# Edge filters of every second four steps computed inside the one-head attention instead of in the filter stage

## The reference

```python
out_i = xw[etype, dst]
out_j = xw[etype, src]
alpha = leaky_relu(out_i @ Q + out_j @ K, 0.2)
alpha = _segment_softmax(alpha, dst, n)
msg = (out_j.reshape(-1, heads, out_ch) * alpha[..., None]).reshape(-1, heads * out_ch)
return segment_sum(msg, dst, num_segments=n) + b
```

```python
h1 = h @ aw_W + aw_b
C = 0.5 * (cos(edge_weight * (PI / CUTOFF)) + 1.0)
Wf = ssp(ssp(edge_attr @ m1_W + m1_b) @ m2_W + m2_b)      # ssp(x) = softplus(x) - log 2
Wf = Wf * C[:, None]
msg = h1[src] * Wf
agg = segment_sum(msg, dst, num_segments=n_nodes)
```

## Time and profile before

| | |
|---|---|
| median of three runs | 6127.67 us (6123.48 to 6130.93) |
| profiled execution, span from first to last instruction | 6128.0 us |
| busy: PE / DVE / ACT / POOL | 4062 / 3143 / 1987 / 3556 us |
| narrow attention, from its first `cuts` to its last add | 3485 to 4151 us |
| filter stage, from its first gather to its last add | 4338 to 5265 us |

### The profile page before, as it was taken

One profiled execution on the slowest core, in us unless ns is written; L12 is line 12 of the kernel. 1 busy time (PEld: TensorE's weight loads), 2 busy tenths in 40 slices (PEclk: granted clock), 3 DMA queues, 4 the chain that ended last, 5 costly groups with the idle time before them and its releaser, 6 DMA issues. The chain is left out here.

```text
span 6128.0 us, 77751 instructions
## 1 busy us (share of the span) xinstructions
PE 4062.0 (66%) x17164; PEld 2958.9 (48%) x17165; DVE 3143.4 (51%) x7175; ACT 1987.0 (32%) x4687; POOL 3556.1 (58%) x2851
## 2 busy tenths in 40 slices
PE   5599922596777769677677444445688888745553
PEld 5488811353555555355556333333455555533332
DVE  5577636522555542355554344445477777533334
ACT  0122200000665541266563122220477777400000
POOL 0244411277777725677773788865555555478884
PEclk9999966798887879788787655557799999866555
DMA  0000002234665534566552233333234343243332
GB/s 7 24 10 10 10 27 61 77 77 94 172 168 154 158 89 92 135 171 166 153 156 61 62 84 83 84 79 89 71 102 103 103 104 103 79 101 84 84 84 73
DMA packets 511546, 558.56 MB, mean 91 GB/s; under 512 B 302820, under 2 KB 394959, under 8 KB 511005
## 3 DMA queue, kind: packets, MB, share of 16 engines
q0 software_dynamic: 349600, 362.07, 24.5%
q1 hardware_dynamic: 158408, 187.29, 10.7%
q10 hardware_dynamic: 3250, 6.40, 0.4%
HBM read 460.45 MB, written 92.22 MB: 90 GB/s over the span
## 5 line engine op out<-in xcount | busy, mean ns | idle before, releaser
L1259 POOL DMA_INDIRECT sum_gx_sb<-scratch_xw,keep_k_row_step_sb x1272 | 1602.7, 1260 | 469.9 <-issue 351.3
L1372 PE MATMUL sum_a_ps<-sum_gx_sb,sum_sel_sb 125*125 125x258 f32 (+1 forms) x4320 | 1214.4, 445 | 539.5 <-ACT sum_gx_sb L1308 218.9
L1372 PEld LDWEIGHTS sum_a_ps<-sum_gx_sb,sum_sel_sb 125*125 125x125 f32 x4320 | 936.1, 242 | 732.2 <-issue 514.1
L1308 ACT ACTIVATE sum_gx_sb<-sum_gx_sb,sum_wt_sb 125x129 f32<-125x129 f32 x3312 | 981.8, 388 | 561.5 <-DVE sum_wt_sb L1501 527.2
L2473 POOL DMA_INDIRECT filter_gx_sb<-scratch_h,keep_k_src_step_sb x424 | 513.5, 1211 | 410.6 <-DVEq L2620 299.0
L1168 POOL DMA_INDIRECT scratch_grouped<-keep_k_value_sb,keep_k_place_sb x400 | 481.7, 1204 | 272.6 <-issue 137.1
L2917 POOL DMA_INDIRECT source_gx_sb<-scratch_h,source_grouped_sb x424 | 527.5, 1244 | 140.4 <-issue 117.5
L2929 PE MATMUL source_s_ps<-source_gx_sb,source_sel_sb 125*125 125x257 f32 x848 | 370.0, 612 | 310.8 <-DMA source_gx_sb<-scratch_h,source_grouped_sb 310.8
L2929 PEld LDWEIGHTS source_s_ps<-source_gx_sb,source_sel_sb 125*125 125x125 f32 x848 | 246.3, 304 | 434.5 <-issue 172.1
L2527 PE MATMUL filter_ps<-filter_m_sb,filter_h_sb 128*125 128x256 f32 x1728 | 403.9, 387 | 15.6 <-DVE filter_f_sb L2592 15.3
L2527 PEld LDWEIGHTS filter_ps<-filter_m_sb,filter_h_sb 128*125 128x125 f32 x1728 | 318.2, 189 | 141.9 <-issue 98.2
(11 more groups left out here) (513 smaller groups left out, 6861.5 us busy)
## 6 DMA issues: line engine op xcount, KB each, us to landing
scratch_hots<-sum_cuts_sb SPq DMA_DIRECT2D x108, 244.1 KB
filter_sel_sb<-scratch_hots SPq DMA_DIRECT2D x106, 244.1 KB
sum_gx_sb<-scratch_xw,keep_k_row_step_sb POOLq DMA_INDIRECT x1272
scratch_xw<-gate_xsb_sb SPq DMA_DIRECT2D x50, 253.9 KB
scratch_xw<-attend_xsb_sb SPq DMA_DIRECT2D x25, 507.8 KB
filter_ea_sb<-in_ea_t SPq DMA_DIRECT2D x436, 24.4 KB
filter_gx_sb<-scratch_h,keep_k_src_step_sb POOLq DMA_INDIRECT x424
source_gx_sb<-scratch_h,source_grouped_sb POOLq DMA_INDIRECT x424
```

The costliest lines, as they stand in the source:

```text
L1259: nc.gpsimd.indirect_dma_start(out=gx[:, q, j, :], out_offset=None, in_=table, in_offset=bass.IndirectOffsetOnAxis(ap=keep["row_step"][:, ...
L1308: last = nc.scalar.activation(here, here, ACT.Copy, scale=wt[q][:, h, j:j + 1])
L1372: last = mm(psa[b][0:P, half, 0:BF], sel[:, 0, p, j, :], gx[:, q, at, half * BF:(half + 1) * BF], **flags)
```

## The change

Half of the edge filters move. `PAIRS` = 106 pairs of steps (steps 4 to 7 of each eight, as two pairs) get their filters in the narrow attention, a pair in each of its 108 parts; SP stores them to a new buffer in HBM, `scratch_wf`. The filter stage then works in 53 turns of eight steps: the first four get their filters as before, the second four load theirs (`wf`).

In the narrow attention the pipeline for pair c is: SP loads its attributes two parts ahead (`filter_load`), PE makes the hidden layer of pair c and the filters of pair c - 2 after the sums of a part and before the link of the score chain (`filter_products`), ACT makes the logarithms of the hidden layer of c and the filters of c - 3 (`filter_logs`), two of a block's three sets before the exponential `weights(s + 1)` and one behind it, DVE makes the softplus sides of c - 1 and c - 4 and the bias of c - 2 after the part's add (`filter_sides`), and SP stores pair c - 5 (`filter_store`). The weights are loaded at the stage's start, and again in the filter stage as before. The loops of all engines in this stage now go over PEEL = 6 blocks, with six blocks ahead of the loop and six behind it. ACT loads one function table, with Exp and Ln, at the stage's start.

```diff
+def filter_products(nc, pe, fl, i, c):
+    mm, P2 = nc.tensor.matmul, 2 * P
+    if pair_runs(i, c):
+        pe.wait_ge(fl["e_in"][c % 3], i * (32 * ROUND_PAIRS // 3) + 32 * (c // 3 + 1))
+        if c >= 2:
+            pe.wait_ge(fl["h1_made"], i * ROUND_PAIRS + c - 1)
+        for o in range(2):
+            last = mm(fl["psh"][c % 2][:, o * P2:(o + 1) * P2], fl["m1"][0:51, 128 * o:128 * o + 128], fl["ea"][0:51, c % 3, :],
+                      start=True, stop=True)
+        last.then_inc(fl["hid"], 1)
+    u = c - 2
+    if pair_runs(i, u):
+        pe.wait_ge(fl["h1_made"], i * ROUND_PAIRS + u + 1)
+        if u >= 1:
+            pe.wait_ge(fl["f2_made"], i * ROUND_PAIRS + u)
+        for j in range(2):
+            for b in range(2):
+                last = mm(fl["psf"][0:P, j * D:(j + 1) * D], fl["h1"][u % 2][:, b * P2 + j * P:b * P2 + j * P + P], fl["m2"][:, b, :],
+                          start=(b == 0), stop=(b == 1))
+        last.then_inc(fl["filt"], 1)
+def filter_sides(nc, dve, fl, i, c):
...
+        vec.scalar_tensor_tensor(fl["h1"][u % 2][:], fl["psh"][u % 2][:, 0:4 * P], 0.0, fl["lgh"][u % 2][:], ALU.max,
+                                 ALU.add).then_inc(fl["h1_made"], 1)
...
+        vec.scalar_tensor_tensor(here, here, 0.0, fl["lgf"][u % 2][:], ALU.max, ALU.add).then_inc(fl["f_made"], 1)
...
+        dve.wait_ge(fl["filt"], i * ROUND_PAIRS + u + 1)
...
+            def block_with_filters(s, q, i, c, last=False):
+                scale(s, q)
+                filter_logs(nc, act, fl, i, c)
+                filter_logs(nc, act, fl, i, c + 1)
+                if not last:
+                    weights(s + 1)
+                filter_logs(nc, act, fl, i, c + 2)
...
                     with pe.If(tiles[p] > NT - 1):
                         sums(s, q, p, False)
+                    if filters is not None:
+                        filter_products(nc, pe, fl, filters[0], filters[1] + p)
                     if ahead:
```

In the filter stage the node rows get four buffers of four steps (`used` was raised by every product, and the gathers now wait for it three groups back), the hidden layer one PSUM buffer instead of two, the products and the segment sums two buffers each. The DVE turn:

```diff
+            def turn(n, i, q):
+                dve.wait_ge(log2_made, n + 1)
+                vec.scalar_tensor_tensor(f2[q][:], f2[q][:], 0.0, lg2[q][:], ALU.max, ALU.add)
...
+                vec.tensor_tensor(ms[0][:], f2[q][:], gx[:, 2 * q], ALU.mult)
...
+                dve.wait_ge(w_in[q], (i + 1) * 16)
+                vec.tensor_tensor(ms[1][:], wf[q][:], gx[:, 2 * q + 1], ALU.mult)
...
+                    make_f2(n + 2, q)
...
+                    make_h1(n + 3, 1 - q)
+                for k in range(2):
+                    dve.wait_ge(summed, 2 * n + k + 1)
+                    for j in range(HF):
+                        here = agg[:, bass.ds(tiles[k * HF + j], 1), 0:D].rearrange("p o f -> p (o f)")
+                        vec.tensor_tensor(here, ps3[k][0:P, j, :], here, ALU.add)
+                        dve.drain()
+                    dve.nop().then_inc(added, 1)
```

More of the change, by code:

```diff
@@ L2460, in filter_sum, with turns_of, runs @@
          "f2_made", "log2_made", "ms_made", "summed", "added"))
-    x_in, e_in, hot_in = ([mem.sem(f"{n}{q}") for q in range(2)] for n in ("x", "e", "hot"))
+    x_in = [mem.sem(f"x{q}") for q in range(4)]
+    e_in, hot_in, w_in = ([mem.sem(f"{n}{q}") for q in range(2)] for n in ("e", "hot", "w"))
     vec, mm = nc.vector, nc.tensor.matmul
-    TURNS, U2 = STEPS // (2 * HF), 2 * HF
+    U2 = 2 * HF
+    TURNS = STEPS // U2
+    LOOPS = (TURNS - 5) // 2
+    def turns_of(engine, turn):
+        with engine.Fori(0, LOOPS) as i:
+            for q in range(2):
+                turn(2 * i + q, i, q)
+        for n in range(2 * LOOPS, TURNS):
+            turn(n, n // 2, n % 2)
+    def runs(n, ahead):
+        return not isinstance(n, int) or n + ahead < TURNS
     with nc.Block() as block:
@@ L2600, in _ @@
             dve.drain()
-            for sem in (ea_free, added, used, used):
-                dve.nop().then_inc(sem, 1)
+            dve.nop().then_inc(ea_free, 1)
+            for k in range(2):
+                dve.nop().then_inc(added, 1)
             dve.wait_ge(landed, 16 * 4)
@@ L2608, in _ @@
             make_f2(1, 1)
[L2609 to L2629 removed]
+            turns_of(dve, turn)
 def nodes_filter(nc, mem, dr, keep, agg):
```

360 lines of the change are left out of this document (253 added, 107 removed).

## The result

The changed kernel takes 6139.24 us (median of 9 runs, 6123.13 to 6150.67), the kernel before, beside it, 6123.48 (6105.99 to 6131.16): a ratio of 1.0023 with a 95% interval of 1.0012 to 1.0033. The change makes the kernel slower by 0.2%. The forecast was 6010, faster, with a range up to 6110, so it was wrong in sign, and the time lies outside the range.

What follows compares the result with a forecast made beforehand. GpSimd was taken to bound the narrow attention, PE with ScalarE and VectorE the filter stage. 6128.0 - 257 (filter stage) + 140 (narrow attention) = 6011, taken as 6010 us; own range 5960 to 6065, wider range 5930 to 6110.

Steps and rivals of the forecast that it cites:

- What bounds which stage: After the change VectorE's chain sets the narrow attention's blocks, 22.6 us over GpSimd's 19.0; GpSimd bounds the filter stage.
- Clock in the narrow attention: PE's granted clock there, 0.50 before, was expected mostly full with drops to half, about 0.8.
- Plain blocks of the narrow attention: Added per block: 5.85 us of VectorE operations, -0.4 for rarer loop jumps, 0.45 for late links.
- Parts with separate tiles: Narrow attention: in 15 of 108 parts VectorE waits for late filter products, 1.5 to 3.6 us each, 0.8 a block.
- +140: Forecast lengthening of the narrow attention in us, from 666 to 803 plus 3 for pairs still under way.
- GpSimd's pace and the loads in the filter stage: Gathers of 1.211 us, 12.1 us per eight-step turn, stage -257 us; the dismissed slower-gather case made it 29 us longer.
- lie beside this: Filter stage: loads of stored filters and one-hots, issued a turn or two ahead, were taken to run alongside the engines' work.
- about 4371 as now: Filter stage: time at which the first product is done, taken as unchanged, freeing the first buffer near 4372.5.
- A: Rival: narrow attention's additions hide almost wholly in GpSimd's pace, 20 us a block, +49, time 5920; chance 9%.
- B: Rival: PE stays at half clock and bounds the narrow attention, 26.5 us a block, +279, time 6150; chance 11%.
- C: Rival: filter stage gains less as PE, VectorE and loads interfere, 13.4 us a turn, time 6080; chance 12%.
- lower bound of +4 us: Narrow attention's smallest lengthening, if all but GpSimd's pace is hidden.

Runs made afterwards that it cites:

- e4: Changed kernel with PE's filter products ahead of a part's sums and VectorE's three operations ahead of its add: 6059.35 us, ratio 0.9902.
- e5: Kernel before, with every part of the narrow attention summed and added as one tile, output not the reference's: 6117.0 us.
- e7: Changed kernel, with no VectorE instruction in the filter stage that has two SBUF inputs, values meaningless: 6126.88 us.
- e11: Changed kernel, in the filter stage both no VectorE instruction with two SBUF inputs and 32-column loads of stored filters and one-hots: 6105.75 us.
- e8: Changed kernel, with filter-stage loads of stored filters and one-hots cut to 32 columns, values meaningless: 6132.68 us.
- e1: Kernel before with only the new filter stage, which loads other data of the same size as stored filters: 5904.24 us.
- e6: Changed kernel, with every part of the narrow attention summed and added as one tile, output not the reference's: 6001.62 us.
- e12: e4 with every part of the narrow attention summed as one tile, output not the reference's: 5965.69 us.
- e9: e4 with the filter stage's start reordered, encoded edges of turns 2 and 3 loaded before turn 1's filters and one-hots: 6048.52 us, ratio 0.9886.

## Why the prediction was wrong

- **What bounds which stage**: right. VectorE's wait for gathers went, GpSimd waits for sums, and in the filter stage the gathers became the bound. Clock in the narrow attention 0.73, forecast near 0.8.
- **Plain blocks of the narrow attention**: right. 5.85 - 0.4 + 0.45 = 5.9 us was forecast to be added, 5.7 was.
- **Parts with separate tiles: the step that failed.** The prediction saw that PE waits there for VectorE's adds, and priced the late products at "1.5 to 3.6 us", 0.8 a block. The wait was 3.9 to 4.8 us in all 16 such parts, 4.6 in the mean, and a block with such a part grew by 12.2 - 5.7 = 6.5 us more than a plain one. The term was wrong in three places. It took a price between the two clocks, where every one of these parts got its products at half clock or near it. Its half-clock price was misread: it took half of the 6.18 us at 4353.86, but the granted clock in that stretch was 0.59, so part of it ran at full clock; at 0.50 the two sets of products took 5.7 us together, not 4.9. And it left out the 0.4 us from the last add to PE's start. In the table, the waits for engines grew by 3.7 us more than in a plain block (+4.1 against +0.4). The idle time without a releaser grew by 1.9 us more (issue: +2.4 against +0.5), as in the 3.10 us ahead of the first of four adds, 1.39 before; and 0.9 of the 6.5 us are in neither column. The causes of these two stay open. (6.5 - 1.8) x 15 / 34 = 2.1 us a block, where 1.8 is what 0.8 a block makes in each of the 15; with 0.4 of waits for gathers, 22.6 becomes 25.1, and 24.9 was measured. Over 35 blocks that is the 79 us between +140 and +219. e4 shows that it is the place of the products and not their amount: moved ahead, they give 22.5 us.
- **GpSimd's pace and the loads in the filter stage: failed too, by 53 us in all.** The prediction cited the rule of the Trainium skill (SBUF — State Buffer, section Who interferes with whom), that a VectorE instruction with two SBUF inputs contends with a GpSimd instruction that reads SBUF, and set it aside because gathers of 1.211 us stood "beside such instructions". 47 of 380 even began inside one, but at its very start, where it is VectorE that waits; a few hundredths of a microsecond later they would have been lengthened, as in e5. Once GpSimd is the bound they start anywhere. The runs agree with the rule (e7, e11). In sum the gathers grew by 424 x (1.275 - 1.211) = 27 us, near the 29 that the prediction had worked out for this case and dismissed. From the first product on, the stage took 672.9 us, where 669.5 - 32.8 = 636.7 was forecast. The same stretch takes 655.9 with gathers undisturbed (e7), 674.2 with small loads (e8) and 636.4 with both (e11): so the second step that failed beside the 1.211 us is that the loads "lie beside this". Neither edit alone gives back the 36 us, and the same code takes 662 to 663 in e1, e4, e6 and e12, so how they divide is not shown. The other 17 us are the start: the forecast took the first product at "about 4371 as now", but SyncE issues loads of filters and one-hots ahead of edges that PE needs; reordered in e9, 10 of the 17 come back. The timeline of PE, kernel after:

```profile
4592.28 3.70 PE L2743 MATMUL filter_ps<-filter_ea_sb,filter_m_sb 51*128 51x500 f32 x4 [9.05 <-DMA filter_ea_sb<-in_ea_t]
```

- **The rivals.** A did not happen. B gave the right time by the wrong way: its clock is there in the parts with separate tiles but not over the stretch (0.73), and a block takes 24.9 us in the mean, not 26.5. C's mechanism is there in part (the loads cost up to 0.4 us a turn), at 12.75 us and not 13.4; what the range lacked was C and a dear narrow attention together.
- **Small sums.** The lower bound of +4 us in the narrow attention does not follow from the forecast's own formula, which gives 35 x 19.0 + 12 + 3 - 666 = +14. ScalarE's 3.7 us a part was 3.9. Neither bears on the result.

Both errors point the same way, 79 + 53 = 132 us of the 134 between 6010 and the span of 6143.9.

## What to carry to other kernels

Work put into the idle time of an engine must be followed at the rare form of the loop's body, and not only at the usual one: here the 15 blocks with separate tiles lost 15 x 10.2 = 153 us, the 19 others 19 x 2.5 = 48. Work that depends on nothing of the present step belongs ahead of the waits and not behind them; the same instructions, moved by a few lines, turned 0.2% slower into 1.0% faster (e4). A price at half clock is read from a row whose whole stretch was granted half clock, and not from one in which the clock rose. An instruction's duration read where another engine releases it holds only as long as it is released so: it may stand 0.01 us short of a conflict, and when it becomes the bound, it runs free.
